# Perceiver, two layers: normalisations and first feed-forward projections issued inside the attentions' last rounds

## The reference

```
x = x + L0_xattn(LN(x), ctx)          # 16 heads, biases
x = x + L0_attn(LN(x))                # 16 heads, relative position bias, sigmoid gate
x = x + L0_ffn(LN(x))
x = x + L1_xattn(LN(x), ctx)
x = x + L1_attn(LN(x))                # 16 heads, causal, Pluecker-line bias
x = x + L1_ffn(LN(x))
```

```
act_qdq(x): scale = max(max(|x|) / 32767, 1e-12); clip(round(x / scale)) * scale
x = act_qdq(x); up = act_qdq(x @ Wu'); gate = act_qdq(x @ Wg')
gate = act_qdq(gate * u16(sigmoid(gate))); o = act_qdq(gate * up); return o @ Wd'
```

## Time and profile before

| | |
|---|---|
| median of 3 runs | 1579.0 us (1577.23 to 1583.18) |
| the profiled execution | 1576.78 us, span 1575.0 us |
| TensorE busy / weight loads | 1459.0 us (93%) / 1127.3 us |
| VectorE, ScalarE, GpSimd busy | 895.5, 713.0, 503.2 us |
| granted TensorE clock, mean | 0.985 |

### The profile page before, as it was taken

How to read it: one execution, slowest core, us unless ns; L and a number is a source line. 1 busy time by engine, 2 the same in 40 slices (tenths; PEclk the granted TensorE clock), 3 DMA queues, 4 the chain that set the end, 5 groups by cost and what they waited for, 6 DMA issues and landing times.

```text
span 1575.0 us, 33033 instructions
## 1 busy us (share of the span) xinstructions
PE 1459.0 (93%) x12564; PEld 1127.3 (72%) x12564; DVE 895.5 (57%) x1889; ACT 713.0 (45%) x1764; POOL 503.2 (32%) x697
## 2 busy tenths in 40 slices
PE   6999997997999999999997888699999999999998
PEld 5877775445777777777775666368858886886887
DVE  5988996479546666666665888443234224323332
ACT  6887775398635555555553656222212212211221
POOL 2445551001026966965656777100000000000000
PEclk9999998999999999999998999899999999999999
DMA  8000000006132162145210000113413430431230
GB/s 299 21 7 2 1 0 21 0 0 194 48 120 69 53 241 72 54 160 220 60 40 1 2 0 0 47 47 140 154 47 105 163 120 30 158 140 60 94 140 14
DMA packets 60510, 123.99 MB, mean 79 GB/s; under 512 B 5008, under 2 KB 15760, under 8 KB 57872
## 3 DMA queue, kind: packets, MB, share of 16 engines
q1 hardware_dynamic: 60432, 122.94, 22.4%
HBM read 108.24 MB, written 14.68 MB: 78 GB/s over the span
## 4 chain that ended last, share of the span: by engine, by line
PE 69%; DVE 15%; POOL 8%; issue 4%; ACT 2%; DVEq 0%; DMA 0%; SPq 0%; POOLq 0%; ACTq 0%
PE ps L944 23%; PE ps L537 15%; PE ps L543 5%; PE ps L741 5%; PE ps L735 4%; PE ps L995 4%; PE ps L761 3%; PE ps L713 3%; POOL R L1968 2%; DVE R L1367 2%; DVE R L1664 2%; POOL R L1950 2%; PE ps L772 2%; DVE amax L1538 2%; POOL R L1942 1%
## 5 line engine op out<-in xcount | busy, mean ns | idle before, releaser
L944 PE MATMUL ps<-R 128*128 128x256 f32 x1792 | 388.6, 379 | 3.5 <-DVE R L1805 3.5
L944 PEld LDWEIGHTS ps<-R 128*128 128x128 f32 x1792 | 340.0, 190 | 52.3 <-issue 6.5
L537 PE MATMUL ps<-R 128*128 128x128 f32 (+1 forms) x1344 | 306.8, 388 | 6.0 <-DVE R L1534 4.3
L537 PEld LDWEIGHTS ps<-R 128*128 128x128 f32 x1344 | 190.2, 194 | 118.7 <-issue 109.5
L1239 ACT ACTIVATE R<-ps,c_nmx 128x257 f32<-128x257 f32 x256 | 118.1, 474 | 126.4 <-DVE c_nmx L1688 126.4
L1950 POOL TENSOR_TENSOR R<-R,c_inv 128x1024 f32<-128x1024 f32 x64 | 121.0, 1891 | 130.6 <-DVE c_inv L1699 130.6
L1664 DVE COPY R<-ps 128x512 f32<-128x512 f32 x128 | 88.2, 689 | 81.9 <-PE ps L761 80.6
L741 PE MATMUL ps<-x_wv,R 128*128 128x256 f32 x512 | 121.1, 379 | 0.0
L2041 POOL TENSOR_SCALAR g_ve<-g_mv 128x4 f32<-128x4 f32 x4 | 0.9, 236 | 345.5 <-DVE g_mv L1767 345.5
L741 PEld LDWEIGHTS ps<-x_wv,R 128*128 128x128 f32 x512 | 92.5, 190 | 10.1
L735 PE MATMUL ps<-R,x_wk 128*128 128x256 f32 x384 | 95.7, 391 | 0.0
(11 more groups left out here) (211 smaller groups left out, 2518.9 us busy)
## 6 DMA issues: line engine op xcount, KB each, us to landing
R<-quadrant_sums SPq DMA_DIRECT2D x32, 1024.0 KB, 6.8
R<-in_f_hq SPq DMA_DIRECT2D x32, 768.0 KB, 4.6
R<-in_ctxT SPq DMA_DIRECT2D x64, 257.0 KB, 2.7
R<-in_f_hq SPq DMA_DIRECT2D x8, 1024.0 KB, 8.3
quadrant_sums<-R SPq DMA_DIRECT2D x8, 1024.0 KB, 8.3
R<-in_ctxT SPq DMA_DIRECT2D x16, 256.0 KB, 3.9
k_ahead<-R SPq DMA_DIRECT2D x16, 256.0 KB, 3.9
R<-k_ahead SPq DMA_DIRECT2D x16, 256.0 KB, 3.1
```

The costliest lines, as they stand in the source:

```text
L537: r = mm(dst, w[:, ki, fo * P:(fo + 1) * P], src[:, ki, :], start=(ki == 0), stop=(ki == KI - 1))
L944: r = mm(ps[:, 4 * (g % 2) + bk, half * HALF:(half + 1) * HALF], f_wr[g % 3][:, w, ki * P:(ki + 1) * P], src[:, k, ki, :], start=(ki == 0) ...
```

## The change

`run_lanes` gets a table `between`: calls that are placed behind a named slot of the last round ("last") or of the tail ("tail"). Where it is given, the last round of the last stage is written out, and the loop has two rounds instead of three.

In `L0_ffn`: twelve tiles are normalised by ScalarE, the last four by VectorE. The first twelve statistics are aggregated behind slot 16 of the last round; GpSimd makes their roots behind its last step of the attention; four tiles are normalised behind slots 4 and 5 of the tail and eight behind the tail; the maximum is taken by groups of four tiles, two of the four groups in the tail. TensorE turns the first weight matrix (12 transposes) in the tail. The maximum over the partitions is no longer GpSimd's: VectorE multiplies the identity by the column of maxima, TensorE multiplies it with a matrix of ones, VectorE takes the maximum of the result. The normalised tiles lie in other memory.

In `L1_ffn`: block 0's statistics, aggregate and normalisation, its turn, copies and the first three of its eight groups of projections are placed in the last round and the tail of A1. The normalised block and its turned copy lie in other memory, and block 0 is turned into banks 0 and 1.

```diff
+                    if between and (name, slot) in between:
+                        between[name, slot]()
...
+                apart = between and steps is stages[-1][1]
...
-                with eng.Fori(1, NT) as i:
+                with eng.Fori(1, NT - 1 if apart else NT) as i:
                     a_round(i, steps, i - 1, steps)
+                if apart:
+                    a_round(NT - 1, steps, NT - 2, steps, "last")
...
# TensorE
+            def turn_weights(m, k):
+                pe.wait_ge(wT_quant, 3 * (NT - 1) + m + 1)
+            def first_weights():
+                for l in range(2):
+                    pe.wait_ge(s["x_updated"], tile(2 * NT - 1, l))
+                turn_weights(F0_WEIGHTS[0], 0)
+            ... ("tail", 4): first_weights
...
             for b in range(NB):
-                pe.wait_ge(f0_xn if b < NB // 2 else f0_xna, TPB * (b % (NB // 2) + 1))
+                if b < NB - 1:
+                    pe.wait_ge(f0_xna, TPB * (b + 1))
+                else:
+                    pe.wait_ge(f0_xn, TPB)
+                    pe.wait_ge(f0_scale, 1)
...
+                if b == 1:
+                    pe.wait_ge(f0_pmax, 1)
+                    mm(ps[:, 7, 0:P], x_ones, x_spread, start=True, stop=True).then_inc(f0_xT, 1)
...
+            def g_pair(b, o, i):
+                if i == 0:
+                    if o == 0:
+                        pe.wait_ge(g_xTc, 2 * b + 2)
+                    if b == 0 and o < NL:
+                        pe.wait_ge(s["x_updated"], tile(3 * NT - 1, o))
...
+                      {("tail", 3): lambda: g_turn(0),
+                       ("tail", 6): lambda: g_pair(0, 0, 0), ("tail", 10): lambda: g_pair(0, 0, 1),
+                       ("tail", 13): lambda: g_pair(0, 1, 0), ("tail", 15): lambda: g_pair(0, 1, 1),
+                       ("tail", 17): lambda: g_pair(0, 2, 0), ("tail", 19): lambda: g_pair(0, 2, 1)})
# ScalarE
+                      {("tail", 4): lambda: f0_normal(0, 2), ("tail", 5): lambda: f0_normal(2, 4)})
+            f0_normal(4, 3 * TPB)
...
+                (18, a_keys), (23, a_exp), (24, a_pT), (27, a_oT))])], {("tail", 6): lambda: g_turned(0)})
# VectorE
+                      {("last", 16): lambda: f0_aggregate(0, 3 * TPB), ("tail", 7): lambda: f0_group_max(0),
+                       ("tail", 12): lambda: f0_group_max(1)})
...
+            f0_aggregate(3 * TPB, T)
+            f0_group_max(2)
+            link(dve, dve_link, v.memset(x_ones, 1.0))
+            dve.wait_ge(f0_rstd, 3)
+            for t in range(3 * TPB, T):
+                v.tensor_scalar(xall[t], x[:, t, :], f_mv[:, t, 0:1], f_rstd[:, t:t + 1],
                                 ALU.subtract, ALU.mult).then_inc(f0_xn, 1)
+            f0_group_max(3)
+            dve.wait_ge(f0_xmax, NB)
+            link(dve, dve_link, v.tensor_reduce(pmax[:, QX:QX + 1], xmax[:, :], AX.X, ALU.max))
+            v.tensor_scalar(x_spread, ident[:], pmax[:, QX:QX + 1], None, ALU.mult).then_inc(f0_pmax, 1)
+            dve.wait_ge(f0_xT, 2 * KI + 1)
+            link(dve, dve_link, v.tensor_reduce(allmax[:, QX:QX + 1], ps[:, 7, 0:P], AX.X, ALU.max))
...
+            def two_stats(t):
+                dve.wait_ge(s["x_updated"], tile(2 * NT, NL - 1))
+                g_stat(0, t)
+                g_stat(0, t + 1)
...
+                      {("last", 4): lambda: two_stats(0), ("last", 11): lambda: two_stats(2),
+                       ("last", 14): lambda: g_aggregate(0), ("last", 27): lambda: g_normalise(0)})
# GpSimd
+            f0_rsqrt(0, 3 * TPB)
...
+            f0_rsqrt(3 * TPB, T)
-            for k in (QX, QG, QU, QS):
+            for k in (QG, QU, QS):
                 all_max(k)
...
+            run_lanes(pool, SLOTS1, [(lambda: None, [
+                (14, of_last(lines)), (17, lambda l, i: b_bias(A1, l, i)), (18, of_last(lines_unit))])],
+                      {("last", 18): lambda: g_rsqrt(0)})
```

More of the change, by code:

```diff
@@ L348, in perceiver, with run_lanes, a_round @@
         SLOTS0, SLOTS1 = 20, 28
-        def run_lanes(eng, slots, stages):
+        def run_lanes(eng, slots, stages, between=None):
             lag = slots // NL
-            def a_round(i, steps, i_behind, steps_behind):
+            def a_round(i, steps, i_behind, steps_behind, name=None):
                 for slot in range(slots):
@@ L902, in p_turn_last @@
                     pe.wait_ge(c_x, T)
-                if not (l < 2 and isinstance(n, int)):
+                if not (l < 2 and isinstance(n, int) and n == NORM[A1]):
                     p_turn(kind, l, n)
             def p_project_last(kind, l, n):
-                if not (l < 2 and isinstance(n, int)):
+                if not (l < 2 and isinstance(n, int) and n == BASE[A1]):
                     p_project(kind, l, n)
[L911 to L920, removed]
             def g_turn(b):
@@ L1105, in attention, with f0_normal @@
                          for at, step in steps])
+            def f0_normal(t0, t1):
+                act.wait_ge(f0_rstd, 2)
+                for t in range(t0, t1):
+                    af(xall[t], x[:, t, :], ACT.Identity, scale=f_rstd[:, t:t + 1], bias=f_nmr[:, t:t + 1])\
+                        .then_inc(f0_xna, 1)
             run_lanes(act, SLOTS0, [
@@ L1120, in _ @@
             gates, ups = ug[:, NF0:, :], ug[:, 0:NF0, :]
[L1121 to L1124, removed]
             act.wait_ge(f0_scale, 1)
             for k in range(KI * NB):
-                act.wait_ge(f0_xT, k + 1)
+                act.wait_ge(f0_xT, k + 1 + (k >= 2 * KI))
                 af(xqT[k // KI][:, k % KI, :], ps[:, k, :], ACT.Identity, scale=qinv[:, QX:QX + 1],
@@ L1513, in enter_a0, with f0_aggregate, f0_group_max @@
                 dve.wait_ge(in_w["nat"], 48)
+            def f0_aggregate(t0, t1):
+                dve.wait_ge(f0_stats, t1)
+                for t in range(t0, t1):
+                    v.bn_aggr(f_mv[:, t, :], f_stats[:, t, :]).then_inc(f0_mv, 1)
+            def f0_group_max(b):
+                if b < NB - 1:
+                    dve.wait_ge(f0_xna, TPB * (b + 1))
+                else:
+                    dve.wait_ge(f0_xn, TPB)
+                v.tensor_reduce(xmax[:, b:b + 1], xgroup[b], AX.XY, ALU.max, apply_absolute_value=True).then_inc(f0_xmax, 1)
             run_lanes(dve, SLOTS0, [
@@ L1750, in of_last, with g_stat, g_aggregate @@
                 return at_tile
-            run_lanes(dve, SLOTS1, [(lambda: None, [(at, of_last(step)) for at, step in (
-                (3, d_slots), (8, d_lines), (8, d_turn_values), (13, d_keys), (16, d_mask),
-                (16, d_max), (17, d_shift), (18, d_sums), (22, d_norm_out), (26, d_add))])])
-            for l in range(NL):
-                dve.wait_ge(s["x_updated"], tile(3 * NT - 1, l))
             xb = x[:, :, :].rearrange("p (b t) d -> p b t d", t=TPB)
-            def g_norm(b):
-                for t in range(TPB):
-                    v.bn_stats(g_stats[:, t, :], xb[:, b, t, :]).then_inc(s["stats_ready"], 1)
+            def g_stat(b, t):
+                v.bn_stats(g_stats[:, t, :], xb[:, b, t, :]).then_inc(s["stats_ready"], 1)
+            def g_aggregate(b):
                 dve.wait_ge(s["stats_ready"], NORMS + TPB * b + TPB)
@@ L1837, in g_last @@
                     v.tensor_tensor(xb[:, b, t, :], xb[:, b, t, :], f_y[:, t % 2, :], ALU.add).then_inc(g_x, 1)
-            g_norm(0)
+            run_lanes(dve, SLOTS1, [(lambda: None, [(at, of_last(step)) for at, step in (
+                (3, d_slots), (8, d_lines), (8, d_turn_values), (13, d_keys), (16, d_mask),
+                (16, d_max), (17, d_shift), (18, d_sums), (22, d_norm_out), (26, d_add))])],
+                      {("last", 4): lambda: two_stats(0), ("last", 11): lambda: two_stats(2),
+                       ("last", 14): lambda: g_aggregate(0), ("last", 27): lambda: g_normalise(0)})
+            for l in range(NL):
+                dve.wait_ge(s["x_updated"], tile(3 * NT - 1, l))
             for b in range(NB):
@@ L2031, in of_last @@
                 return at_tile
-            run_lanes(pool, SLOTS1, [(lambda: None, [
-                (14, of_last(lines)), (17, lambda l, i: b_bias(A1, l, i)), (18, of_last(lines_unit))])])
-            for l in range(NL):
-                pool.wait_ge(s["x_updated"], tile(3 * NT - 1, l))
             def g_rsqrt(b):
```

126 lines of the change are left out of this document (65 added, 61 removed).

## The result

| | before | after |
|---|---|---|
| median (lowest to highest) | 1578.12 us (1577.15 to 1583.18), 4 runs | 1558.84 us (1557.34 to 1561.14), 4 runs |
| the profiled execution | 1576.78 us, span 1575.0 | 1561.14 us, span 1559.4 |

A forecast was written before the change was run, and what follows sets the result against it. TensorE is busy 93% of the span, so time was to be won at its waits at two feed-forward heads: -8.4 - 8.9 = -17.3 us from 1576.8, plus 2.2 to the median, gives 1561.7 us, between 1553 and 1570.

The forecast's parts named there:

- First head: Start of L0_ffn: scale 6.0 us earlier plus 2.4 from the upper clock, -8.4 us, bounds -4 to -9.8.
- rival 2: Both heads: the clock does not hold at the blocks' starts or the first transposes; 1567.5 us, chance 0.20.
- TensorE's way: L0_ffn's start: 24 transposes 3.7 us, copy 0.6, 16 transposes 2.5, product with ones 0.4, maximum and scale 0.6.
- the attention's end: Ahead of L0_ffn: taken as unmoved at 253.0, since the 0.89 us of aggregates meet an existing stall; ends -0.4 and +0.9.
- The rule of exclusion between VectorE and GpSimd: Attention's tail before L0_ffn: a GpSimd power excluding VectorE could add up to 1.4 us; no charge taken.
- Second head: Start of L1_ffn behind A1: block 0's norm, turn and three of eight groups moved earlier; -8.9 us, bounds -14.6 to -5.
- GpSimd's wait and the clock behind it: A1's last round: GpSimd's root waits for VectorE's aggregate, 3.7 us remaining, then 1.5 for the lower clock.
- normalisation ahead of lane 3's lines: A1's last round: VectorE's normalisation of block 0 delays the last power by 1.45 us.
- dense stretch to the third group: A1's tail on TensorE: 5.58 us old work, 1.1 last projection, 10.3 six moved projections; 17.0 us.
- GpSimd's wait costs nothing: Rival, A1's last round: GpSimd arrives later or its next work has slack; 1556.5 us, chance 0.15.
- Hidden further on: Rival: gains at both heads vanish in later work and nothing stays; 1577 to 1579 us, chance 0.07.
- Written-out rounds slower: Rival, last round of each attention: code fetched for one use runs slower; 1589 to 1629 us, chance 0.06.

The follow-up runs named there:

- kernel 1: Changed kernel with all that was put into A1's last round and tail taken back, written-out rounds kept: 1570.17 us, ratio 0.9952 to the kernel before.
- kernel 3: Changed kernel with GpSimd's root of block 0 seven slots later, behind slot 25 instead of 18 of the last round: 1551.60 us.
- kernel 7: Kernel 3 with block 0's normalisation moved from the last round to behind slot 1 of the tail, after lane 3's lines: 1550.96 us.
- kernel 2: Kernel before with only the last round of the two self-attentions written out instead of looped, no work moved: 1578.01 us, ratio 1.0001.
- the change again: Kernel 5: the changed kernel with no edit, run again beside the following three kernels: 1558.58 us.
- kernel 8: Changed kernel with the edits of kernels 6 and 7 together: 1551.38 us, ratio 0.9835 to the kernel before.
- kernel 6: Changed kernel with TensorE's product with ones ahead of the transposes of blocks 0 and 1 instead of behind them: 1557.52 us.
- kernel 4: Changed kernel without block 0's six projections in A1's tail; they come behind the attention, norm and turn stay: 1565.49 us.

## Why the prediction was right

*First head, -8.4 forecast.* The steps are right; the sizes fit in part by luck. The inverse of the second scale that the block makes is 6.6 us earlier in the trace than before. With the 1.4 to 1.5 us that the execution had lost ahead of the head, most of them near 114 us, the gain is 8.0 to 8.1, and the kernel with this head alone gives 8.0. Of it 5.9 lie at the first scale (6.0 forecast) and 2.1 in the block's first products (2.4 forecast), which ran at 2.4 GHz; so what rival 2 put at risk there came in.

Two errors hide in the 5.9. TensorE's way from the first of the 24 transposes to the scale was taken at 7.8 us and took 8.5, as the lower clock lay over nearly all of them (4.88 us, forecast 3.7); at full clock, in kernel 1, it took 6.7. And the attention's end, taken as unmoved, came 0.6 us earlier against what stood ahead of it: its adds into x are 1.38 us later than before near 228 us (227.89 against 226.51), the last one 0.80 (252.89 against 252.09).

VectorE's way was right: 5.1 us from the aggregates to the spread column, 5.0 forecast. That TensorE's transposes decide and not VectorE is shown by the 2.51 us wait at 261.41 for this execution; at full clock the two ways end within 0.2 us of each other (kernel 1: column at 258.04, product with ones at 258.27).

The rule of exclusion between VectorE and GpSimd, on which no charge was taken for the power of 128x12, is left open for this place: the L1508 of 241.58 (L1478 in the prediction) was over before the power of 242.27 began, so nothing in the tail tests it.

*Second head, -8.9 forecast, 10.8 to 11.0 in the trace and 11.3 by kernel 1.* The mechanism is right in each step, the sizes too pessimistic, all on one side:

| step | forecast | measured |
|---|---|---|
| GpSimd's wait and the clock behind it | 3.7 + 1.5 = 5.2 | 3.5 + 0.9 = 4.4 (kernel 3 gives the same 4.4 back) |
| normalisation ahead of lane 3's lines | 1.45 | 1.3 (lane 3's keys 9.37 behind lane 2's, before 8.03; kernel 7 gives 0.8 of it back) |
| dense stretch to the third group | 17.0 | 15.9 |

The term that was mis-sized most is the dense stretch. The tail's old work was taken at 5.58 us, its busy time where each step stands alone. In a dense program the next step begins before the last has drained: L636 at 990.88 takes 0.60 us, and the projection behind it begins after 0.43. Next comes the clock: behind the wait it was 0.53 for 3.6 us only, and cost 0.9 instead of 1.5.

*The rivals.* That GpSimd's wait costs nothing is refuted by the 13.02 us between lanes and by kernel 3. That the clock does not hold came true in part only, for the weights' transposes and after the stall, not in the blocks. Hidden further on: refuted, the 15.6 us that the traces are apart behind the second head stay 15.6 to the end. Written-out rounds slower: refuted by kernel 2.

*Open.* Why kernel 3 gains 2.8 us more than its place explains. Against the first trace of the change, all that it gains beyond the 4.4 lies ahead of the stall. Against the trace of the change again it is 9.0 us shorter: 2.9 ahead of the stall, 4.4 at it, and 1.7 at the fall near 989, which neither the first trace of the change nor kernels 3, 7 and 8 have. Whether the stall brings that fall in most executions no run shows. For the same reason differences under 2 us between kernels 3, 7 and 8 are not settled.

## What to carry to other kernels

A step that is moved into a dense program should be placed by the queue of each engine that it passes: a root of 1.3 us stood in front of work that was ready, waited 4.23 us for a result that another engine made later, and cost 4.4 us; seven slots later it cost nothing. Long independent products belong between the short dependent steps of a tail, where 8.6 us of them lengthened it by 3.2. When two engines' ways to one result end close together (0.2 us apart here at full clock), reordering one of them only swaps the wait.

## What was not expected of the hardware

The granted clock falls in some executions and not in others, at a price of 1.5 and 1.7 us in the two cases worked out above. The places recur: the fall where A0 begins, near 114 us in the changed kernel's trace, is in those of kernels 1, 2, 6 and 8 as well, and that in the last product of `L0_ffn`, near 401, in those of kernels 2, 4, 5 and 7. The kernel before and kernel 3 have neither. A difference of two profiled executions is to be read against these falls before it is put down to a change, and best by stretches: instructions that both traces share show where it arose.

VectorE and GpSimd hold each other in both directions. Before, VectorE ended behind GpSimd; here GpSimd ends late. Its timeline near 239 us:

```profile
239.06 2.33 POOL L1952 TENSOR_TENSOR R<-R,mask_hr 128x1024 f32<-128x1024 f32 x1 [2.74 <-ACT R L1087]
```

beside which VectorE ran this, with both inputs from SBUF:

```profile
239.15 0.49 DVE L1514 TENSOR_TENSOR R<-R,wsc 128x384 f32<-128x384 int16 x1
```

GpSimd's product takes 2.33 us instead of 1.89: 0.44 more, about the 0.49 that VectorE had. In the trace of the kernel before the same two instructions met the other way: GpSimd's began 0.29 us ahead of VectorE's (237.69 and 237.98) and took 1.89, and VectorE's took 2.02, to 0.42 behind GpSimd's end. Here it began 0.09 ahead. The eight traces of kernels with the new first head all have the 2.33, and the kernel with only the rounds written out has the 2.02 again. So 0.2 us less between the two starts goes with another engine being held. With it the lane's add into x came 6.35 us behind that of the lane before instead of 7.06, which is a part of the 0.6 us by which the attention's end came earlier.
